# Attention steps in another order: scores three steps ahead, maxima turned one step earlier, the mask added by TensorE in 156 of 256 steps

## Chip, core and metric

The kernel runs on one core of one Trainium2 chip. The metric is the device time of one execution in microseconds (us): the time of the whole launch, of which the profile's span, from the first to the last instruction, is all but a microsecond or two. Smaller is better. A "granted clock" of 1.00 in the profile is TensorE at 2.4 GHz, 0.50 is 1.2 GHz.

## What is computed

The input `x` has 8 batches of 512 tokens with 512 features. A layer norm is followed by a cross attention with 16 heads of 32 features over a context of which the causal mask leaves the first 512 rows; then a second layer norm and a routed feed forward follow.

```python
def attention(q, latent_kv, Wq, Wkv_expand, Wout):      # per batch
    qp = q @ Wq.T
    k, v = jnp.split(latent_kv @ Wkv_expand.T, 2, axis=-1)
    scores = jnp.einsum('bhqd,bhkd->bhqk', qh, kh) * inv_sqrt_d
    scores = jnp.where(causal, scores, jnp.finfo(scores.dtype).min)
    attn = jax.nn.softmax(scores, axis=-1)
    out = jnp.einsum('bhqk,bhkd->bhqd', attn, vh)
    return out @ Wout.T

x = x + attention(layernorm(x), ctx, Wq, Wkv_expand, Wout)
x = x + ffn(layernorm(x))      # router softmax over 8 experts per output, two best, weighted
```

The change touches the attention alone.

## The kernel before

**Work and order.** Every engine has its program written out by hand; semaphores tie the programs together. The attention is a chain of 32 groups, four to a batch: group c of batch b (`n = 4b + c`) is four heads. A group has eight **steps** v = 0 to 7 (`UNITS`), and all five engines walk through the same steps. I call steps 0 to 4 the head of a group and steps 5 to 7 its tail. After the last group come the router and the experts, to which nothing is changed.

**Two passes of scores.** The softmax needs the maximum of each row before its exponentials. So the scores are computed twice. *First pass* (`scores`, L621): one step covers one block of 128 queries and two heads, and fills the two halves of the PSUM tile `pair0` (`s_ps`), one half a head. Widths go down as the steps of the target group go up: targets 0 and 1 are 512 keys wide, 2 and 3 are 384, 4 and 5 are 256, 6 and 7 are 128. VectorE (`maxima`, L1286) adds the mask tile `future` and takes the maximum in one custom instruction for each head, which is followed by an instruction that reads the accumulator into a column of `nmax`. The next use of a half waits for that (`negmax`). `target(c, v)` says for which step of a later group step v computes first-pass scores: `LEAD` = 2 steps ahead of one group's distance. So at step 5 the last scores (target 7) of group n+1 are issued, and at step 6 the first ones of group n+2.

**Turning the maxima.** When group n+1 has its 16 columns of maxima, TensorE turns them (`turn_maxima`, L630, into the PSUM tile `ps5`, which also holds the sums `d_ps`). ScalarE takes the rounded part (`hi_shift`, L964, `nm_h`), VectorE the rest (`lo_shift`, L1295, `nm_l`). SyncE puts both by DMA (L342) into two rows of the stack `qk_st` of group n+1. This happens at `TURN` = step 6. Step 0 of group n+1 waits for these rows (`rows_in`).

**Second pass** (`shifted_scores`, L648): keys by queries, two heads a step, into `pair1`, with the maximum already subtracted by those two rows. ScalarE takes the exponentials (L1023) into `pT`. GpSimd zeroes the diagonal's upper part (L1738, `causal`) and adds the blocks up for the sums (L1725, L1730, `added`). TensorE multiplies with the values (L661, step 6 and 7 and step 1 of the next group: `finish_group`) and forms the sums (L673, and L681 in `finish_group`, behind the last addition of GpSimd).

**Work of other kinds in the same steps.** Queries (steps 0, 2, 3, 4) and keys (`key_step`: step 5 for c = 0 and 3, step 6 for c = 1 and 2) are made three groups ahead, each in three matmuls (L262, L263, L264: high by high, low by high, high by low), and split by ScalarE (L956) and VectorE (L1270 queries, L1273 keys). In group 0 the values and the turning of the next batch's tokens (L570, L1261) come in. The output projection of the batch before, 16 chunks of three matmuls, lies at c = 1, 2 and 3 (`out_block`); after the fourth chunk of a token block VectorE adds the residual (L1322, `x1_ok`), and the next user of that PSUM bank waits for it. `refined` (L1301, L1303, step 3) and `scaled` (L1309, step 4) are VectorE's normalisation of the group before. `STATISTICS` are the steps in which VectorE takes the layer norm's statistics for two batches ahead (L1227) and GpSimd the scales from them (L1692 to L1702). `NORMALISED` are the steps in which ScalarE applies them (L988). `SPLIT` has ScalarE and GpSimd split the outputs (L971, L1683).

Batch 0 has no output projection, batches 1 to 6 are alike, and batch 7 has nothing ahead.

## Time and profile before

| | us |
|---|---|
| median of 3 runs | 2108.45 (2106.45 to 2109.36) |
| the profiled execution | 2109.9 |
| its span | 2108.2 |
| TensorE busy, and its share of the span | 2001.4 (95%) |
| VectorE, ScalarE, GpSimd busy | 1464.4, 1044.2, 851.9 |
| first to last second-pass step of the attention | 56.2 to 677.9 |
| batches 1 to 6 of the attention | 125.48 to 598.62, 473.14 in all, 78.86 each |
| from 677.92 to the end | 1430.28 |

The profile gives, for each engine, busy time and, for a group of like instructions, what ended the idle time before them. PE is TensorE, PEld its loading of weights, DVE is VectorE, ACT ScalarE, POOL GpSimd, SPq the issues of DMAs by SyncE. Matmuls overlap: one of 512 columns shows about 0.40 us, while the next begins 0.23 us after it; so a busy share near 100% is not the same as no time to gain, and starts are to be compared rather than durations.

### The profile page before, as it was taken

The numbers are of one execution on the slowest core, as the hardware profiler recorded it, in microseconds if no ns is written. First come the engines' busy times: TensorE is split into PE (matmuls) and PEld (weight loads), VectorE is DVE, ScalarE is ACT, GpSimd is POOL, SyncE is SP. The second block draws the span as 40 slices with busy tenths as digits, with TensorE's granted clock in tenths as the row PEclk, the third lists the DMA queues.
The fourth block names the chain that finished last, engine by engine and source line by source line (L and its number), as shares of the span: only waits on it lengthen the run. The fifth ranks groups of instructions, "written<-read, shape, count | busy, mean of one in ns | idle before, by whom it ended". The sixth has DMA issues, their size and how long they took to land.

```text
span 2108.2 us, 31128 instructions
## 1 busy us (share of the span) xinstructions
PE 2001.4 (95%) x9822; PEld 1522.9 (72%) x9872; DVE 1464.4 (69%) x3268; ACT 1044.2 (50%) x2093; POOL 851.9 (40%) x985
## 2 busy tenths in 40 slices
PE   5899998999986899999999999999999999999999
PEld 3566666665663677777777777778888888888887
DVE  5766666766665667777778777657877878778533
ACT  2665565565554246767676776733433334333300
POOL 3676666676666334435344345202311113111100
PEclk8999999999997999999999999999999999999999
DMA  5454454454353545455445455472322222222110
GB/s 155 117 126 111 131 130 112 130 135 115 102 148 120 192 159 204 162 192 184 164 175 207 150 189 187 154 269 81 109 95 75 77 92 93 106 80 75 60 40 31
DMA packets 99220, 275.85 MB, mean 131 GB/s; under 512 B 13435, under 2 KB 14480, under 8 KB 95030
## 3 DMA queue, kind: packets, MB, share of 16 engines
q1 hardware_dynamic: 94518, 216.16, 32.3%
q10 hardware_dynamic: 4608, 58.72, 8.1%
q14 instruction: 69, 0.57, 0.1%
q8 instruction: 25, 0.41, 0.1%
HBM read 131.67 MB, written 92.27 MB: 106 GB/s over the span
## 4 chain that ended last, share of the span: by engine, by line
PE 85%; DVE 4%; DMA 3%; POOL 2%; SPq 2%; issue 2%; ACT 1%; ACTq 0%; POOLq 0%; DVEq 0%
PE pair L262 21%; PE pair L264 20%; PE pair L263 20%; PE ps L262 3%; PE pair L621 3%; PE pair L648 3%; PE ps L661 3%; PE ps L264 3%; PE ps L263 3%; PE pair L859 2%; DVE pair L1286 1%; SPq L356 1%; DMA qk_st<-nm_l 1%; PE ps L681 1%; DVE xr L1322 1%
## 5 line engine op out<-in xcount | busy, mean ns | idle before, releaser
L262 PE MATMUL pair<-w_h,hT 128*128 128x512 f32 x1920 | 797.1, 415 | 3.5 <-DVE xb L1620 1.9
L264 PE MATMUL pair<-w_h,hT 128*128 128x512 f32 x1920 | 751.7, 392 | 0.0
L263 PE MATMUL pair<-w_l,hT 128*128 128x512 f32 x1920 | 747.6, 389 | 0.0
L1811 POOL TENSOR_TENSOR logits<-logits,second 128x512 f32<-128x512 f32 x224 | 298.4, 1368 | 609.0 <-DVE second L1499 608.7
L264 PEld LDWEIGHTS pair<-w_h,hT 128*128 128x128 f32 x1920 | 360.6, 188 | 80.2
L263 PEld LDWEIGHTS pair<-w_l,hT 128*128 128x128 f32 x1920 | 361.6, 188 | 74.7
L262 PEld LDWEIGHTS pair<-w_h,hT 128*128 128x128 f32 x1920 | 363.3, 189 | 71.4 <-issue 2.3
L1286 DVE CUSTOM_DVE_ANT_0 pair<-pair,future 128x256 f32<-128x256 f32 (+3 forms) x512 | 245.3, 508 | 159.5 <-PE pair L621 156.4
L1620 DVE SCALAR_TENSOR_TENSOR xb<-pair,c_now,xb 128x512 f32<-128x512 f32 x256 | 191.9, 750 | 190.4 <-PE pair L264 183.2
L1023 ACT ACTIVATE pT<-pair,zero 128x1024 f32<-128x1024 f32 (+3 forms) x256 | 202.4, 791 | 220.2 <-PE pair L648 212.3
L621 PE MATMUL pair<-qk_st 96*128 96x256 f32 (+3 forms) x512 | 164.5, 358 | 29.6 <-DVE nmax L1286 25.9
L1692 POOL TENSOR_TENSOR rstd<-moments,eps 128x1 f32<-128x1 f32 x64 | 33.0, 516 | 324.9 <-DVE moments L1237 297.1
L1738 POOL TENSOR_SCALAR_AFFINE_SELECT pT<-pT 128x256 f32<-128x256 f32 x256 | 109.0, 427 | 129.5 <-ACT pT L1023 129.5
L621 PEld LDWEIGHTS pair<-qk_st 96*128 96x128 f32 x512 | 101.1, 198 | 75.2 <-DVE nmax L1286 36.0
L1553 DVE SCALAR_TENSOR_TENSOR scrap<-ps,w 128x512 bf16<-128x512 f32 x224 | 153.2, 684 | 0.8 <-ACT w L1119 0.8
L648 PE MATMUL pair<-qk_st 98*128 98x256 f32 (+3 forms) x512 | 132.1, 342 | 22.2 <-DMA qk_st<-nm_l 16.8
L1092 ACT ACTIVATE over<-over 128x512 f32<-128x512 f32 x224 | 141.7, 633 | 7.1
L1547 DVE SCALAR_TENSOR_TENSOR ps<-logits,ps 128x512 f32<-128x512 f32 x192 | 133.3, 694 | 17.0 <-DVE scrap L1553 0.5
L1089 ACT ACTIVATE junk<-over 128x512 bf16<-128x512 f32 x224 | 141.5, 632 | 7.1
L1116 ACT ACTIVATE w<-tree 128x512 f32<-128x512 f32 x32 | 20.3, 633 | 239.7 <-DVE tree L1501 239.7
L1730 POOL TENSOR_TENSOR acc<-acc,pT 128x512 f32<-128x512 f32 (+1 forms) x124 | 128.7, 1038 | 10.3
L1084 ACT ACTIVATE over<-logits 128x512 f32<-128x512 f32 x224 | 129.6, 623 | 0.4
(166 smaller groups left out, 2784.0 us busy)
## 6 DMA issues: line engine op xcount, KB each, us to landing
logits<-lg_all ACTq DMA_DIRECT2D x32, 1792.0 KB, 7.5
qk_st<-qk SPq DMA_DIRECT2D x384, 128.0 KB, 2.3
lg_all<-ev_a SPq DMA_DIRECT2D x32, 768.0 KB, 5.6
lg_all<-ev_b SPq DMA_DIRECT2D x32, 768.0 KB, 3.3
xb<-x SPq DMA_DIRECT2D x64, 256.0 KB, 3.2
hT_all<-hT SPq DMA_DIRECT2D x32, 512.0 KB, 3.6
hT<-hT_all SPq DMA_DIRECT2D x32, 512.0 KB, 3.7
...
```

The costliest lines, as they stand in the source:

```text
L262: pe.matmul(dst, lh, rh, start=start, stop=False)
L263: pe.matmul(dst, lh, rl, start=False, stop=False)
L264: return pe.matmul(dst, ll, rh, start=False, stop=stop)
L621: pe.matmul(s_ps[:, j, 0:w], qk_st[c][0:STACK, 0, hh, i * P:w], qk_st[c][0:STACK, 1, hh, 0:w], start=True, stop=True).then_inc(s["scores"], 1)
L648: mm = pe.matmul(dst[:, j, 0:w], qk_st[c][0:STACK + SHIFT_ROWS, 1, hh, kb * P:(kb + 1) * P], qk_st[c][0:STACK + SHIFT_ROWS, 0, hh, kb * P: ...
L1023: act.activation(pT[kb][:, pair:pair + 2, :], src[:, :, 0:S - kb * P], ACT.Exp, bias=zero[:])\
L1089: act.activation(junk[:], over[j][:], ACT.Sign, accum_out=sign_sum[:, i, e:e + 1])\
L1092: act.activation(over[j][:], over[j][:], ACT.Tanh, scale=0.5, accum_out=tanh_sum[:, i, e:e + 1]).then_inc(s["first_step"], 1)
L1286: dve.tensor_tensor_reduce(row, row, future[:, S - (i + 1) * P:S], -1.0, -MASKED, ALU.add, ALU.min, accum_out=nmax[:, c % 2, at:at + 1]).t ...
L1553: dve.scalar_tensor_tensor(scrap[:, e % 2, :], taken_ps[e % 2], 1.0, w2[:], ALU.min, ALU.mult, accum_out=c_taken[:, i, e - 1:e]).then_inc( ...
L1620: dve.scalar_tensor_tensor(xb[i][:], l_ps[e % 4], c_now[i][:, e:e + 1], xb[i][:], ALU.mult, ALU.add).then_inc(s["acc"], 1)
L1811: pool.tensor_tensor(logits[t % 2][:, e - 1, :], logits[t % 2][:, e - 1, :], second[:], ALU.subtract)\
```

## The change

- `LEAD` goes from 2 to 3: first-pass scores run three steps ahead. The last of group n+1 (target 7) are issued at step 4, those of group n+2 begin at step 5.
- `TURN` goes from 6 to 5, and TensorE turns the maxima at the end of the step, behind that step's scores. ScalarE's `hi_shift` stays with it, behind a key split of the same step; VectorE's `lo_shift` comes at the beginning of step 6.
- In 156 steps (all eight with c = 0, steps 1 to 4 otherwise) the mask is added by TensorE: behind the score matmuls of both heads come two matmuls of 128 columns, one a head, with `ident_r` and `mask_r`, into the diagonal block. There both heads are issued together, and VectorE takes both maxima by one `tensor_reduce` over both halves. The other steps (5, 6, 7 and 0 with c = 1, 2, 3, targets 0 to 3) keep the custom instructions, with head 0 at the end of a step and head 1 in the next.
- The two halves of `refined` go to steps 3 and 4, `scaled` to the beginning of step 5. The keys for c = 0 and 3 are made right behind the second-pass scores of step 5, ahead of its scores.
- The output projection's blocks begin at (c, step) = (1, 0), (1, 6), (2, 3), (3, 0) instead of (1, 0), (1, 4), (2, 0), (3, 0) (unchanged in the last batch); the residual addition comes one step after the last chunk. One store of a sum goes from SyncE's part of c = 2 to that of c = 3.
- `STATISTICS` go from (1, 5), (2, 1), (2, 5), (3, 1) to (2, 1), (3, 0), (3, 1), (3, 2), and one of the normalisations from (2, 5) to (3, 6).

```diff
-LEAD = 2
+LEAD = 3
+        def masked(c, v):
+            return c == 0 or target(c, v)[1] >= QB
-        TURN = 6
+        TURN = 5
+        WEIGHTED = 6
-        STATISTICS = ((1, 5), (2, 1), (2, 5), (3, 1))
-        NORMALISED = ((2, 5), (3, 1), (3, 5), (3, 7))
+        STATISTICS = ((2, 1), (3, 0), (3, 1), (3, 2))
+        NORMALISED = ((3, 1), (3, 5), (3, 6), (3, 7))
-        SCALED = 4
+        SCALED = 5
+        OUT_FIRST = ((1, 0), (1, 6), (2, 3), (3, 0))
+        OUT_FIRST_LAST = ((1, 0), (1, 4), (2, 0), (2, 4))
...
-                    pe.matmul(s_ps[:, j, 0:w], ..., start=True, stop=True).then_inc(s["scores"], 1)
+                    mm = pe.matmul(s_ps[:, j, 0:w], ..., start=True, stop=not mask)
+                    if not mask:
+                        mm.then_inc(s["scores"], 1)
+                if mask:
+                    for j in heads:
+                        pe.matmul(s_ps[:, j, i * P:w], ident_r[:], mask_r[:], start=False, stop=True)\
+                            .then_inc(s["scores"], 1)
...
                 if some(n - 1):
-                    pe.wait_ge(s["o_ok"], n - 1)
+                    pe.wait_ge(s["refined"], 2 * (n - 1))
                 pe.transpose(r_ps, nmax[:, c % 2, :], ident[:]).then_inc(s["turned"], 1)
...
+                if mask:
+                    at = 2 * pair * QB + i
+                    dve.wait_ge(s["scores"], 2 * u + 2)
+                    dve.tensor_reduce(nmax[:, c % 2, at:at + QB + 1:QB], s_ps[:, :, 0:(i + 1) * P], AX_X, ALU.max,
+                                      negate=True).then_inc(s["negmax"], 2)
...
                     for v in range(UNITS):
-                        if v == TURN and (more or c < KC - 1):
+                        if v == TURN + 1 and (more or c < KC - 1):
                             lo_shift(n + 1)
-                        if v == key_step(c) == TURN and ahead:
+                        if not (first and c == 0) and v == SCALED:
+                            scaled(n - 1, (c - 1) % KC)
+                        if v == key_step(c) and ahead:
                             lo_of(n + AHEAD, KL, "k", key_bank(c))
...
-                            maxima(n + g, (c + g) % KC, vv)
+                            maxima(n + g, (c + g) % KC, vv, masked(c, v))
-                            if v == REFINED:
-                                refined(n - 1, (c - 1) % KC)
-                            if v == SCALED:
-                                scaled(n - 1, (c - 1) % KC)
+                        if not (first and c == 0) and REFINED <= v < REFINED + 2:
+                            refined(n - 1, (c - 1) % KC, v - REFINED)
```

**VectorE, group c = 3 of batch 5, from the last but one narrow maxima to the split of the turned ones.** In a row, `ISA` with 128x1 reads the accumulator, and `pair0,nmax` is the custom instruction. Before:

```order
L1286 ISA pair0,nmax_81<-pair0,future_84 128x128
L1286 ISA nmax_81 128x1
L1286 ISA pair0,nmax_81<-pair0,future_84 128x128
L1286 ISA nmax_81 128x1
L1309 TENSOR_TENSOR o_sb2_89<-ps4,o_sb2_89 128x512
L1270 SCALAR_TENSOR_TENSOR qk_72<-ps7,qk_72 128x512
L1286 ISA pair0,nmax_81<-pair0,future_84 128x128
L1286 ISA nmax_81 128x1
L1286 ISA pair0,nmax_81<-pair0,future_84 128x128
L1286 ISA nmax_81 128x1
L1273 TENSOR_TENSOR qk_72<-ps6,qk_72 128x512
L1295 TENSOR_TENSOR nm_l_83<-ps5,nm_h_82 16x128
```

and now, from the last narrow maximum (the `TENSOR_REDUCE`) on:

```order
L1305 TENSOR_REDUCE nmax_81<-pair0 128x2
L1350 TENSOR_TENSOR xr_96<-ps6,xr_96 128x512
L1331 SCALAR_TENSOR_TENSOR o_sb2_91<-ps5,o_sb2_91 128x512
L1290 SCALAR_TENSOR_TENSOR qk_72<-ps7,qk_72 128x512
L1337 TENSOR_TENSOR o_sb2_91<-ps4,o_sb2_91 128x512
L1293 TENSOR_TENSOR qk_72<-ps6,qk_72 128x512
L1311 ISA pair0,nmax_81<-pair0,future_84 128x512
L1311 ISA nmax_81 128x1
L1311 ISA pair0,nmax_81<-pair0,future_84 128x512
L1311 ISA nmax_81 128x1
L1320 TENSOR_TENSOR nm_l_83<-ps5,nm_h_82 16x128
```

Between the last maximum of a group and `nm_l` there was one key split; now the residual, the second half of `refined`, the query split, `scaled`, the key split and two maxima 512 wide stand there.

**TensorE, steps 5 and 6 of the same kind of group (c = 3, batch 6).** Before, from the end of step 4 on:

```order
L621 MATMUL pair0<-qk_st0_73 128x128 x2
L648 MATMUL pair1<-qk_st3_76 128x256 x2
L621 MATMUL pair0<-qk_st0_73 128x128 x2
L262 MATMUL ps6<-ctx_h_69,wkv_h_63 128x512
L263 MATMUL ps6<-ctx_l_70,wkv_h_63 128x512
L264 MATMUL ps6<-ctx_h_69,wkv_l_64 128x512
L648 MATMUL pair1<-qk_st3_76 128x128 x2
L661 MATMUL ps4<-pT0_77,v_sb_71 32x512 x4
L630 MATMUL ps5<-ident_49,nmax_81 16x128
```

and now:

```order
L634 MATMUL pair0<-qk_st0_73 128x128 x2
L640 MATMUL pair0<-mask_r_86,ident_r_85 128x128 x2
L667 MATMUL pair1<-qk_st3_76 128x256 x2
L265 MATMUL ps6<-ctx_h_69,wkv_h_63 128x512
L266 MATMUL ps6<-ctx_l_70,wkv_h_63 128x512
L267 MATMUL ps6<-ctx_h_69,wkv_l_64 128x512
L634 MATMUL pair0<-qk_st1_74 128x512
L649 MATMUL ps5<-ident_49,nmax_81 16x128
L667 MATMUL pair1<-qk_st3_76 128x128 x2
L634 MATMUL pair0<-qk_st1_74 128x512
L680 MATMUL ps4<-pT0_77,v_sb_71 32x512 x4
```

The keys stand ahead of the scores, the turn stands ahead of step 6's second-pass scores instead of behind its values, and the scores there are already those of the group after next.

**GpSimd, group c = 3 of batch 5, steps 1 to 3.** `AFFINE_SELECT` is the diagonal of a step, `rstd` and `nmean` the scales. Before:

```order
L1738 AFFINE_SELECT pT0_77<-pT0_77 128x2x128 x2
L1692 TENSOR_TENSOR rstd_53<-moments_52,eps_58 128x1
L1694 TENSOR_TENSOR rstd_53<-rstd_53,minus_half_57 128x1
L1699 TENSOR_TENSOR nmean_54<-moments_52,rstd_53 128x1
L1702 TENSOR_TENSOR nmean_54<-nmean_54,minus_one_55 128x1
L1738 AFFINE_SELECT pT1_78<-pT1_78 128x2x128
L1725 TENSOR_TENSOR acc_86<-pT0_77,pT1_78 128x768
L1738 AFFINE_SELECT pT1_78<-pT1_78 128x2x128
L1725 TENSOR_TENSOR acc_86<-pT0_77,pT1_78 128x768
```

and now, from step 1's scales on:

```order
L1719 TENSOR_TENSOR rstd_53<-moments_52,eps_58 128x1
L1721 TENSOR_TENSOR rstd_53<-rstd_53,minus_half_57 128x1
L1726 TENSOR_TENSOR nmean_54<-moments_52,rstd_53 128x1
L1729 TENSOR_TENSOR nmean_54<-nmean_54,minus_one_55 128x1
L1765 AFFINE_SELECT pT1_78<-pT1_78 128x2x128
L1752 TENSOR_TENSOR acc_88<-pT0_77,pT1_78 128x768
L1719 TENSOR_TENSOR rstd_53<-moments_52,eps_58 128x1
L1721 TENSOR_TENSOR rstd_53<-rstd_53,minus_half_57 128x1
L1726 TENSOR_TENSOR nmean_54<-moments_52,rstd_53 128x1
L1729 TENSOR_TENSOR nmean_54<-nmean_54,minus_one_55 128x1
L1765 AFFINE_SELECT pT1_78<-pT1_78 128x2x128
L1752 TENSOR_TENSOR acc_88<-pT0_77,pT1_78 128x768
```

A second set of scales stands between the two long additions (and a third one, not shown, between the diagonals of steps 0 and 1).

## Rows read from the trace of the kernel before

**Rows 1.** Busy time by stretch: heads and tails of batch 3, then batches 1 to 6.

```profile
core 0: us, PE busy (x) PEld busy (x) DVE busy (x) ACT busy (x) POOL busy (x), PEclk, DMA share, GB/s
285.64:296.89 11.25, 11.25 (x70) 8.55 (x70) 6.19 (x20) 7.96 (x11) 7.75 (x10) 1.00 0.80 210
296.89:304.20 7.31, 7.03 (x58) 4.58 (x58) 5.80 (x19) 4.86 (x11) 6.08 (x9) 1.00 0.09 20
304.20:316.84 12.64, 11.86 (x74) 8.75 (x72) 8.34 (x26) 7.11 (x10) 8.75 (x11) 1.00 0.76 202
316.84:323.96 7.12, 7.12 (x51) 4.56 (x50) 5.48 (x20) 2.50 (x5) 6.26 (x11) 1.00 0.26 86
323.96:335.79 11.83, 11.14 (x70) 8.28 (x69) 7.26 (x25) 5.96 (x8) 3.75 (x8) 1.00 0.67 167
335.79:344.12 8.33, 6.93 (x40) 4.09 (x40) 6.62 (x22) 3.73 (x7) 7.76 (x13) 0.80 0.10 36
344.12:354.99 10.87, 10.87 (x70) 8.36 (x69) 6.73 (x24) 6.67 (x9) 5.06 (x11) 1.00 0.62 144
354.99:363.85 8.86, 5.60 (x40) 2.79 (x40) 6.67 (x21) 5.59 (x11) 8.61 (x10) 1.00 0.12 39
125.48:598.62 473.14, 437.12 (x2761) 300.75 (x2761) 315.75 (x1020) 263.84 (x404) 325.26 (x456) 0.96 0.47 122
```

**Rows 2.** The waits of 125.48 to 598.62: in total, times, longest.

```profile
PE pair L621 <- DVE nmax L1286: 17.2, 15, 1.5
...
PE pair L648 <- DMA qk_st<-nm_l: 7.5, 8, 1.5
PE ps L262 <- DVE xr L1322: 6.9, 12, 0.7
```

**Rows 3.** Timeline of 282 to 364: start, duration, engine, line.

```profile
282.70 0.28 DVE L1295 TENSOR_TENSOR nm_l<-ps,nm_h 16x128 fp32r<-16x128 f32 x1 [1.17 <-ACT nm_h L964]
...
285.64 0.72 PE L648 MATMUL pair<-qk_st 98*128 98x512 f32 x2 [1.01 <-DMA qk_st<-nm_l]
...
356.40 0.29 DVE L1286 CUSTOM_DVE_ANT_0 pair<-pair,future 128x128 f32<-128x128 f32 x1
...
356.86 0.69 DVE L1309 TENSOR_TENSOR o_sb<-ps,o_sb 128x512 f32<-128x512 f32 x1
357.46 0.68 DVE L1270 SCALAR_TENSOR_TENSOR qk<-ps,qk 128x512 fp32r<-128x512 f32 x1
...
359.22 0.28 PE L630 MATMUL ps<-ident,nmax 128*16 128x128 f32 x1
...
360.52 0.28 DVE L1295 TENSOR_TENSOR nm_l<-ps,nm_h 16x128 fp32r<-16x128 f32 x1 [1.04 <-ACT nm_h L964]
360.73 0.68 DVE L1286 CUSTOM_DVE_ANT_0 pair<-pair,future 128x512 f32<-128x512 f32 x1
...
361.98 0.13 DVE L1286 DVE_READ_ACCUMULATOR2_ANT nmax<- 128x1 f32 x1
...
363.85 0.73 PE L648 MATMUL pair<-qk_st 98*128 98x512 f32 x2 [1.30 <-DMA qk_st<-nm_l]
```

**Rows 4.** Timeline of TensorE, 316 to 327: two narrow scores; a projection that waits.

```profile
316.67 0.34 PE L621 MATMUL pair<-qk_st 96*128 96x128 f32 x2
...
325.12 0.40 PE L264 MATMUL ps<-xnT_h,wq_l 128*128 128x512 f32 x1
326.21 0.50 PE L262 MATMUL ps<-wo_h,oT_h 128*128 128x512 f32 x1 [0.69 <-DVE xr L1322]
```

**Rows 5.** VectorE's groups by shape: count, busy, mean ns, idle before.

```profile
L1286 DVE CUSTOM_DVE_ANT_0 pair<-pair,future 128x512 f32<-128x512 f32 x128 | 87.0, 705 | 32.0 <-PE pair L621 31.8
```

**Rows 6.** Timeline of GpSimd in the last group of batch 3.

```profile
351.74 0.19 POOL L1692 TENSOR_TENSOR rstd<-moments,eps 128x1 f32<-128x1 f32 x1 [3.02 <-DVE moments L1237]
...
353.04 0.41 POOL L1738 TENSOR_SCALAR_AFFINE_SELECT pT<-pT 128x256 f32<-128x256 f32 x1
...
366.40 0.73 POOL L1730 TENSOR_TENSOR acc<-acc,pT 128x256 f32<-128x256 f32 x1
```

More of the change, by code:

```diff
@@ L606, in project_out, with scores @@
                     mm.then_inc(s["wo_mm"], 1)
-            def scores(n, c, v, heads=(0, 1)):
+            def scores(n, c, v, heads=(0, 1), mask=False):
                 u = n * UNITS + v
@@ L800, in body @@
                         if more or c + g < KC:
-                            scores(n + g, (c + g) % KC, vv, (0,) if vv < LATE else (0, 1))
-                        if v == key_step(c) != TURN and ahead:
-                            take(key_bank(c), "K", n + AHEAD)
-                            keys((c + AHEAD) % KC, b if c == 0 else b + 1, key_bank(c))
+                            if masked(c, v):
+                                scores(n + g, (c + g) % KC, vv, mask=True)
+                            else:
+                                scores(n + g, (c + g) % KC, vv, (0,))
+                        if v == TURN and (more or c < KC - 1):
+                            turn_maxima(n + 1, c + 1)
             def epilogue():
```

67 lines of the change are left out of this document (36 added, 31 removed).

## The prediction, as written before the changed kernel was run

> **What bounds the kernel now.** I read the stretches of batch 3 first [rows 1], then the waits [rows 2], then the timeline where the waits lie [rows 3, 4]. A batch of the attention takes 78.86 us in the mean of batches 1 to 6 (473.14 / 6), and TensorE is busy for 437.12 of those 473.14 [rows 1]: 36 us of gaps. What follows the attention, some 1430 us, isn't touched. So at most an eighth of the attention, and a fiftieth of the kernel, is open even if every gap goes, save for starts that lie further apart than a dense stream's.
>
> The gaps aren't spread evenly. The four heads (steps 0 to 4) of batch 3 take 11.25, 12.64, 11.83 and 10.87 us, with TensorE busy for 11.25, 11.86, 11.14 and 10.87; the tails (steps 5 to 7) take 7.31, 7.12, 8.33 and 8.86, with 7.03, 7.12, 6.93 and 5.60 [rows 1]. The reader is to see that the tails of c = 2 and 3 hold most of it, and that the granted clock is 0.80 in the tail of c = 2 and 1.00 in the others. The waits name three causes on TensorE: a first-pass score that waits for a maximum (17.2 us), second-pass scores that wait for the maxima's rows (7.5 us in 8 groups), and an output projection that waits for the residual (6.9 us, 12 times) [rows 2].
>
> The timeline shows how the tail of c = 3 ends: the turn at 359.22, the low half done at 360.80, second-pass scores at 363.85 with 1.30 us of idle time for the DMA [rows 3]. **The chain that ends a group is: last maximum, turn, split, two DMAs, next group.** From the end of the low half to the next group it took 3.05 us here and 2.66 a batch earlier (282.98 to 285.64, it waited there too) [rows 3]. I take 2.65.
>
> **Masks on TensorE.** A batch has 20 masked steps, 40 extra matmuls of 128 columns; 312 in all (7 x 40 + 32). Two scores of that width show 0.34 us together [rows 4], while one matmul of 128 moving columns shows 0.28 [rows 3]: so the second starts 0.06 us after the first. 312 x 0.06 = 19 us, 2.4 a batch, on TensorE's stream; nothing where it waits anyway, and 0.17 each (half of the pair's 0.34), 53 us, if they don't follow each other so closely. I take 0.06, since four narrow matmuls now stand in a row. On the other side stand scores one target later in each step: in a head two scores fall from 384 to 256 and two from 256 to 128, about -0.2 us at a column's rate (those of 512 start 0.23 us apart in a dense stream, as said under the profile above). Net per head: +0.25 for c = 1 to 3 (8 masks, 0.48, less 0.23), +0.37 for c = 0 (10 masks). In the tail of c = 0 it is +0.36 for masks and +0.23 for widths.
>
> The Trainium skill, page "TensorE: Matmul & The Clock Gate", section "Back-to-back issue gap", gives about 81 ns for a sustained matmul of 128 columns with its weight load. The rows show 60; by the page the masks would cost 25 us instead of 19.
>
> **Maxima by one instruction.** The trace has no `tensor_reduce`. The nearest rows: the custom instruction takes 0.29 us at 128 and 0.705 at 512 elements [rows 3, 5], so about 1.08 ns an element and 0.15 us fixed. Over both halves that is 0.43 us (2 x 128), 0.70, 0.98 and 1.26 (2 x 512). Today two narrow ones take 0.46 from start to the next start (356.40 to 356.86), two wide ones 1.25 and 0.13 (360.73 to 361.98, then the read) [rows 3]. In starts the gain is 0 to 0.15 us a step: at most 156 x 0.15 = 23 us of VectorE, which has a third of its time free [rows 1]. From above, twice the time per element adds 0.28 to a narrow and 1.1 to a wide one. I take the lower end, since unlike instructions of 512 fp32 elements from PSUM (L1309, L1270, L1286) all take 0.68 or 0.69 us there [rows 3].
>
> The Trainium skill, page "VectorE: DVE Perf Modes", section "Rules for kernel authors", speaks against this part: it calls `tensor_reduce` the slowest VectorE instruction, with a single rate of 1x, and advises to restructure around it. No row here shows it.
>
> **Tails.** Now the turn itself waits for nothing, but `nm_l` stands behind two wide maxima. The chain from the end of step 4 is VectorE's queue: end of the matmul 0.25, last narrow maxima 0.37, then `refined`, query split and `scaled` at 0.60 from start to start (356.86 to 357.46 [rows 3]), two wide maxima 1.25, `nm_l` 0.30: 3.97, and 2.65 of DMA: 6.6. The residual of c = 1 and c = 3 and the key split of c = 3 (and c = 0) add 0.60 each.
> - c = 0: chain 0.25 + 0.37 + 4 x 0.60 + 1.1 (both heads by one instruction) + 0.30 + 2.65 = 7.1; TensorE's own work 7.31 + 0.59 - 0.28 of gap [rows 1] = 7.6. It takes 7.6.
> - c = 1: chain 7.2; own work 7.12 - 0.69 (three of three projections become two) + 0.23 = 6.7. It takes 7.2.
> - c = 2: chain 6.6; own work as for c = 1, 6.7 (two projections, now at steps 5 and 6). It takes 6.7.
> - c = 3: chain 6.6 + 1.2 = 7.8; own work 6.7 less two projections of 0.69, 5.3. It takes 7.8.
>
> Together 29.3 us for 31.6 in batch 3. What is late next is thus VectorE's queue, no longer the wait of a narrow score behind `refined` (17.2 us in six batches), which goes.
>
> **Heads.**
> - c = 0: 11.25 + 0.37 + 0.6 = 12.2. The 0.6 is GpSimd: in batch 3 its last addition of c = 3 ends at 367.13 (366.40 + 0.73) [rows 6], 3.3 us after the next group began, and just when `finish_group` wants it. One more set of scales (351.74 to 353.04, 1.30 us [rows 6]) now stands between the long additions. The two steps before GpSimd's additions have slack, so I put half of the 1.3 on the path.
> - c = 1: 12.64 - 0.69 (step 4's projection) - 0.6 (its wait, 6.9 / 12 [rows 2]) + 0.25 = 11.6.
> - c = 2: 11.83 - 0.86 (the projection's wait, 325.12 to 326.21 less 0.23 [rows 4]) + 0.25 + 0.45 = 11.7. The 0.45 is a new wait: block 2 begins at step 3 behind the residual of step 2 (0.25 + 0.60 + 0.69 + 0.05 = 1.6 after step 2's scores, while TensorE is there after 1.15).
> - c = 3: 10.87 + 0.25 + 0.8 = 11.9. The same wait moves here: block 3 begins at step 0, the residual of block 2 stands behind the maximum of head 1, whose score is issued in that same step 0. Queued behind the waiting projection on TensorE are the first head's score of step 0 and all of step 1.
>
> Together 47.4 for 46.6. **Sum:** 47.4 + 29.3 = 76.7 for 78.86: 2.2 us a batch, 13 in six. Batch 0 has no projection and batch 7 nothing ahead; I put nothing there. The constants `ident_r` and `mask_r` cost GpSimd less than a us while it waits for the first loads. Span 2108.2 - 13 = 2095; the profiled execution (2109.9) lies 1.5 above the median of the runs, 2108.45, so against that median 2095 as well.
>
> **Rivals.**
> - *TensorE's own work becomes the bound.* If VectorE's queue is shorter than I add up, and the residual and GpSimd hold nobody, heads are 11.6 + 11.6 + 11.2 + 11.1 = 45.5 (those above without the 0.6, 0.45 and 0.8) and tails 7.6 + 6.7 + 6.7 + 5.3 = 26.3: 71.8, 7.0 us a batch, 42 in all: 2066. For it: the granted clock of 0.80 in one tail [rows 1] comes back with the gaps. Against: seven VectorE instructions at 0.60 are plain in the new order. Half of what this rival adds would give 2080.
> - *GpSimd ends the last group (slower).* All three sets of scales of 1.3 us now stand in c = 3, behind three statistics for which GpSimd must wait (3.02 us for one today [rows 6]), in front of additions that already end when TensorE asks for them. Two sets more, 2.6, and 1.4 of waiting, all passed on at step 1 of group 0: +4.0 - 2.2 = +1.8 a batch, 11 in all: 2119. It decides as soon as the last addition ends later than 3 us after the next group's begin by more than the tails have gained.
> - *The turn at step 5 brings nothing.* The low half sits behind two wide maxima, and if `tensor_reduce` runs at half the rate of the custom instruction (+0.28 in four chains, +1.1 in c = 0, 2.2 a batch), the gain is used up: 2108. The Trainium skill's rule on `tensor_reduce`, above, points this way.
>
> **How the numbers follow.** Forecast 2095 (2086 to 2106): 0.42. TensorE-bound, 2066 to 2085: 0.18. GpSimd-bound, 2110 to 2125: 0.23. Nothing, 2104 to 2112: 0.17. About 0.2%, 4.2 us, is what a measurement of this kernel tells from no change. Faster: 0.18 + 0.36 of the forecast's 0.42 + 0.03 = 0.57. Same: 0.04 + 0.10 + 0.01 = 0.15. Slower: 0.22 + 0.02 + 0.04 = 0.28. The range that leaves out 0.1 on each side is 2074 to 2119.
>
> **What the changed profile would show.** Batches 1 to 6 at about 76.7 us each, their tails near 7.6, 7.2, 6.7 and 7.8. `nm_l` some 4 to 5.2 us behind the end of step 4, with wide maxima right ahead of it. Waits of first-pass scores for maxima down from 17.2 to a few us; second-pass scores that still wait for the rows. Projection waits in c = 2 step 3 and c = 3 step 0 only. The mask matmuls 0.06 us apart. A `tensor_reduce` of 2 x 128 at 0.43 us. GpSimd's last addition of c = 3 about 0.5 us late. The forecast is wrong if a batch's time changes in the heads rather than in the tails, or if the end of a group hangs on ScalarE, which takes one more normalisation at c = 3, step 6, or on GpSimd.

## The result, and the profile after

The changed kernel takes **2134.73 us** (median of 4 runs, 2127.21 to 2138.16) where the kernel before takes 2108.9 (4 runs): a ratio of **1.0116**, 95% interval 1.0085 to 1.0148. It is slower, beyond the forecast's upper end (2106) and beyond every range that was given a chance (2125). The profiled execution took 2136.3 (span 2134.6). From the last second-pass step (703.95) to the end it is 1430.65 us, for 1430.28 before: the loss is all in the attention. There 1.3 us come before its first step, 1.3 in batch 0, 1.3 in batch 7, and 22.2 in batches 1 to 6 (495.36 for 473.14, 82.56 a batch for 78.86).

Busy time by stretch of the changed kernel: heads and tails of batch 3, then batches 1 to 6 (columns and order as in [rows 1]; the granted clock stands third from the end).

```profile
295.74:308.79 13.05, 12.29 (x80) 9.31 (x80) 4.00 (x7) 8.03 (x12) 10.11 (x14) 1.00 0.71 181
308.79:316.85 8.06, 7.49 (x65) 5.48 (x64) 6.78 (x11) 5.26 (x11) 6.32 (x9) 1.00 0.11 25
316.85:328.46 11.61, 11.46 (x78) 8.87 (x78) 5.60 (x11) 6.20 (x9) 7.33 (x9) 1.00 0.81 210
328.46:338.51 10.05, 8.55 (x47) 4.62 (x47) 6.27 (x15) 3.01 (x6) 6.04 (x9) 0.83 0.21 67
338.51:350.51 12.00, 11.85 (x78) 9.00 (x78) 6.29 (x16) 6.50 (x8) 4.96 (x10) 1.00 0.60 144
350.51:357.70 7.19, 6.63 (x48) 3.86 (x47) 5.59 (x14) 2.48 (x5) 6.48 (x9) 1.00 0.11 36
357.70:369.87 12.17, 11.60 (x78) 9.00 (x77) 7.82 (x24) 6.66 (x9) 5.75 (x15) 1.00 0.62 152
369.87:377.67 7.80, 5.86 (x41) 2.90 (x41) 6.80 (x17) 6.25 (x12) 7.39 (x10) 1.00 0.10 36
...
128.04:623.40 495.36, 457.07 (x3001) 319.93 (x3001) 291.77 (x660) 263.93 (x404) 325.91 (x458) 0.97 0.45 117
```

Two stretches stand out: the head of c = 0 (13.05) and the tail of c = 1 (10.05, granted clock 0.83). The head of c = 0 is 13.69 in the mean of six batches, because batch 1 takes 16.87 there, at a granted clock of 0.80:

```profile
128.04:144.91 16.87, 15.07 (x79) 11.10 (x80) 4.00 (x7) 8.24 (x12) 11.54 (x15) 0.80 0.54 140
```

The means of batches 1 to 6, beside the forecast:

| | heads c = 0, 1, 2, 3 | tails c = 0, 1, 2, 3 | batch |
|---|---|---|---|
| before | 11.76 12.60 11.83 10.89 | 7.29 7.16 8.38 8.96 | 78.86 |
| forecast | 12.2 11.6 11.7 11.9 | 7.6 7.2 6.7 7.8 | 76.7 |
| after | 13.69 11.58 11.99 12.19 | 8.06 10.05 7.24 7.77 | 82.56 |

The waits of TensorE in batches 1 to 6 (in total, times, longest):

```profile
PE ps L680 <- DVE o_sb L1337: 9.8, 18, 0.6
PE ps L265 <- DVE xr L1350: 8.8, 13, 0.9
...
PE ps L649 <- DVE o_sb L1331: 4.2, 6, 0.7
PE ps L680 <- POOL pT L1765: 3.9, 6, 1.7
```

The wait that the forecast wanted gone is gone (first-pass scores for maxima, 17.2 us in [rows 2], now 1.8 in two rows). In its place stands one that the forecast doesn't name: the values' product (L680, step 6), 18 times, which is once in each of c = 0, 1 and 2 of six batches, waits for `scaled` (L1337). The timeline of the tail of c = 1 shows it (start, duration, engine, line, shape, idle before):

```profile
329.07 0.68 DVE L1350 TENSOR_TENSOR xr<-ps,xr 128x512 f32<-128x512 f32 x1
...
329.67 0.68 DVE L1331 SCALAR_TENSOR_TENSOR o_sb<-ps,o_sb 128x512 f32<-128x512 f32 x1
330.27 0.68 DVE L1290 SCALAR_TENSOR_TENSOR qk<-ps,qk 128x512 fp32r<-128x512 f32 x1
...
330.41 0.28 PE L649 MATMUL ps<-ident,nmax 128*16 128x128 f32 x1 [0.70 <-DVE o_sb L1331]
...
330.87 0.68 DVE L1337 TENSOR_TENSOR o_sb<-ps,o_sb 128x512 f32<-128x512 f32 x1
331.46 0.69 DVE L1311 CUSTOM_DVE_ANT_0 pair<-pair,future 128x512 f32<-128x512 f32 x1
331.69 1.93 PE L680 MATMUL ps<-pT,v_sb 128*32 128x512 f32 x8 [0.55 <-DVE o_sb L1337]
...
333.56 0.80 PE L265 MATMUL ps<-ctx_h,wkv_h 128*128 128x512 f32 x1
```

The values of step 6 go into the PSUM tile `ps4`, which `scaled` of the group before still reads. Before, `scaled` ran at the end of step 4; now it is at 330.87 behind the residual, the second half of `refined` and the query split, and TensorE stands. The turn, too, waits for `refined`. Between the two waits TensorE has three small jobs, and then its clock is down: the eight value products take 1.93 us here, for 1.06 at full clock (e1_scaled4, below). The stretches around it, and the same place one batch earlier and one later:

```profile
329.50:331.60 2.10, 0.94 (x5) 0.42 (x4) 2.10 (x5) 0.99 (x3) 2.02 (x3) 1.00 0.32 125
331.60:335.10 3.50, 3.41 (x12) 1.49 (x13) 1.39 (x5) 0.00 (x0) 1.93 (x3) 0.51 0.26 82
335.10:338.50 3.40, 3.40 (x28) 2.22 (x27) 2.01 (x5) 1.07 (x2) 1.14 (x2) 1.00 0.16 36
...
249.80:253.20 3.40, 3.40 (x12) 1.45 (x13) 1.26 (x5) 0.00 (x0) 1.81 (x3) 0.50 0.26 82
...
413.60:417.00 3.40, 3.34 (x12) 1.42 (x13) 1.36 (x5) 0.00 (x0) 1.91 (x3) 0.50 0.31 82
```

TensorE was busy for 0.94 of 2.10 us, and the next 3.4 us run at 1.2 GHz: in every one of batches 1 to 6, at the same place. The kernel before has such stretches too: in the tail of c = 2 in five of the six batches, in that of c = 3 in four, and once in the head of c = 0. In all they are 37.5 us long there and 27.3 us in the changed kernel, so the mean clock of batches 1 to 6 is 0.96 before and 0.97 after.

GpSimd at the end of c = 3 of batch 2 and the head of c = 0 of batch 3, with the TensorE rows that wait for it:

```profile
297.13 0.40 POOL L1765 TENSOR_SCALAR_AFFINE_SELECT pT<-pT 128x256 f32<-128x256 f32 x1
297.62 0.73 POOL L1757 TENSOR_TENSOR acc<-acc,pT 128x256 f32<-128x256 f32 x1
298.31 1.27 POOL L1710 TENSOR_TENSOR oT_l<-o_sb,oT_h 128x512 fp32r<-128x512 f32 x1
299.55 0.40 POOL L1765 TENSOR_SCALAR_AFFINE_SELECT pT<-pT 128x256 f32<-128x256 f32 x1
300.03 0.73 POOL L1757 TENSOR_TENSOR acc<-acc,pT 128x256 f32<-128x256 f32 x1
```
```profile
300.08 0.43 PE L680 MATMUL ps<-pT,v_sb 128*32 128x128 f32 x8 [0.45 <-POOL pT L1765]
300.81 0.85 PE L700 MATMUL ps<-acc,ones 128*32 128x384 f32 x8 [0.31 <-POOL acc L1757]
```

GpSimd has no gap there. Its last addition ends at 300.76, 5.0 us after the group began (295.74), where it was 3.3 before [rows 6]. In batch 1 the values wait 1.67 us for GpSimd at this place, and the next 6.8 us run at 1.2 GHz.

### The profile page after: what moved, and what is told of

Same layout as the page of the kernel before. It is cut to its first block, busy times and chain, and to the rows that moved or that the text cites. A ratio compares the mean times of both kernels' runs of the same rounds, so it can differ in the third digit from the quotient of the medians.

```text
span 2134.6 us, 31419 instructions
## 1 busy us (share of the span) xinstructions
PE 2026.5 (95%) x10134; PEld 1548.6 (73%) x10184; DVE 1431.8 (67%) x2800; ACT 1044.2 (49%) x2093; POOL 852.6 (40%) x987
## 4 chain that ended last, share of the span: by engine, by line
PE 82%; POOL 6%; DVE 5%; issue 2%; DMA 2%; SPq 1%; ACT 1%; POOLq 0%; DVEq 0%; ACTq 0%
PE pair L265 21%; PE pair L267 20%; PE pair L266 20%; PE ps L265 3%; PE ps L680 3%; PE pair L634 3%; PE pair L667 2%; PE ps L266 2%; PE ps L267 2%; PE pair L879 2%; POOL oT_l L1710 1%; POOL acc L1757 1%; POOL acc L1752 1%; POOL pT L1765 1%; PE pair L640 1%
## 5 line engine op out<-in xcount | busy, mean ns | idle before, releaser
L1305 DVE TENSOR_REDUCE nmax<-pair 128x2 f32<-128x256 f32 (+3 forms) x156 | 104.2, 668 | 175.6 <-PE pair L640 175.4
L634 PE MATMUL pair<-qk_st 96*128 96x256 f32 (+3 forms) x512 | 150.5, 346 | 16.8 <-DVE nmax L1311 9.7
L1311 DVE CUSTOM_DVE_ANT_0 pair<-pair,future 128x512 f32<-128x512 f32 (+3 forms) x200 | 121.2, 627 | 49.6 <-PE pair L634 48.0
L667 PE MATMUL pair<-qk_st 98*128 98x256 f32 (+3 forms) x512 | 135.4, 347 | 14.8 <-DMA qk_st<-nm_l 11.9
L634 PEld LDWEIGHTS pair<-qk_st 96*128 96x128 f32 x512 | 95.9, 194 | 67.8 <-DVE nmax L1311 21.5
```

The source lines that it names most:

```text
L634: mm = pe.matmul(s_ps[:, j, 0:w], qk_st[c][0:STACK, 0, hh, i * P:w], qk_st[c][0:STACK, 1, hh, 0:w], start=True, stop=not mask)
L667: mm = pe.matmul(dst[:, j, 0:w], qk_st[c][0:STACK + SHIFT_ROWS, 1, hh, kb * P:(kb + 1) * P], qk_st[c][0:STACK + SHIFT_ROWS, 0, hh, kb * P: ...
```

## Experiments

Each kernel is the changed one with the edit shown, unless it says otherwise. Names like `SCALED` are those of the diff above. All are compared with the kernel before, run on the same chip. The means of batches 1 to 6 of each profiled execution:

| | heads c = 0, 1, 2, 3 | tails c = 0, 1, 2, 3 | batch | time | ratio (95%) |
|---|---|---|---|---|---|
| e1_scaled4 | 13.32 11.57 11.98 12.19 | 7.42 7.57 6.56 8.04 | 78.65 | 2110.2 | 1.0010 (0.9998 to 1.0021) |
| e2_stats | 12.05 11.58 11.98 12.26 | 8.06 9.21 7.31 7.76 | 80.22 | 2123.64 | 1.0073 (1.0056 to 1.0091) |
| e3_blocks | 13.63 12.73 12.17 11.35 | 8.06 7.89 7.33 7.60 | 80.75 | 2124.12 | 1.0082 (1.0062 to 1.0101) |
| e4_nomask | 13.79 10.78 11.27 11.50 | 7.89 8.47 7.18 7.88 | 78.76 | 2111.11 | 1.0014 (1.0002 to 1.0026) |
| e5_scaled_stats | 12.11 11.57 12.08 12.28 | 7.42 7.66 6.78 8.03 | 77.93 | 2107.14 | 0.9999 (0.9988 to 1.0011) |
| e12_masks_custom | 12.06 11.55 12.03 12.26 | 7.41 7.84 6.64 8.16 | 77.96 | 2107.09 | 1.0000 (0.9990 to 1.0009) |
| e9_all_three | 11.57 10.84 11.37 11.58 | 7.08 7.88 6.77 8.60 | 75.68 | 2092.24 | 0.9927 (0.9901 to 0.9953) |
| e8_lead_turn | 11.81 11.71 11.51 10.73 | 7.20 7.31 7.78 7.92 | 75.97 | 2094.84 | 0.9942 (0.9925 to 0.9959) |
| e10_apart | 11.85 11.25 11.37 11.58 | 6.89 7.88 6.66 8.69 | 76.17 | 2092.93 | 0.9931 (0.9915 to 0.9948) |
| e13_residual | 11.99 10.80 11.05 10.74 | 7.30 8.33 6.93 7.96 | 75.09 | 2088.3 | 0.9908 (0.9883 to 0.9934) |
| e11_filler | 13.72 11.57 11.98 12.18 | 8.06 8.54 7.21 7.77 | 81.02 | 2128.34 | 1.0102 (1.0077 to 1.0128) |

### One part undone at a time

**e1_scaled4**: VectorE's normalisation at its old place.

```diff
-SCALED = 5
+SCALED = 4
-    if not (first and c == 0) and v == SCALED:        # at the step's beginning
-        scaled(n - 1, (c - 1) % KC)
-    if not (first and c == 0) and REFINED <= v < REFINED + 2:
-        refined(n - 1, (c - 1) % KC, v - REFINED)
+    if not (first and c == 0):                        # at its end
+        if v == REFINED:
+            refined(n - 1, (c - 1) % KC, 0)
+            refined(n - 1, (c - 1) % KC, 1)
+        if v == SCALED:
+            scaled(n - 1, (c - 1) % KC)
```

> The changed kernel with one part undone: both halves of `refined` at step 3 and `scaled` at the end of step 4, as before, instead of steps 3, 4 and the beginning of 5. Theory V (the values of step 6 wait for `scaled`, which now stands behind the residual, `refined` and the query split; with the hole the granted clock falls in the tail of c = 1 in every batch): the tail of c = 1 goes from 10.05 to 7.2 to 7.5 us, those of c = 0 and 2 lose about 0.5 each, 3.5 to 3.9 a batch, 21 to 23 in all: about 2112. Theory P (GpSimd's additions end the last group late, head of c = 0): that head stays at 13.7 and the time falls by no more than 3. Theory M (the masks on TensorE): no change beyond 3 us.

It takes the ratio from 1.0116 to 1.0010; only e4_nomask has as large an effect. The tail of c = 1 falls by 2.5 us and those of c = 0 and 2 by 0.6 and 0.7. The timeline of the same place (e1_scaled4, batch 3):

```profile
319.96 0.68 DVE L1350 TENSOR_TENSOR xr<-ps,xr 128x512 f32<-128x512 f32 x1
...
320.43 0.27 PE L649 MATMUL ps<-ident,nmax 128*16 128x128 f32 x1
...
320.56 0.68 DVE L1337 TENSOR_TENSOR o_sb<-ps,o_sb 128x512 f32<-128x512 f32 x1
...
321.38 1.06 PE L680 MATMUL ps<-pT,v_sb 128*32 128x512 f32 x8 [0.22 <-DVE o_sb L1337]
```

The turn waits for nothing, the values for 0.22 us, and the clock stays: their eight products take 1.06 us. In batches 1 to 6 the wait of L680 for `scaled` is down from 9.8 to 1.1 us. The four tails are now 7.42, 7.57, 6.56 and 8.04, 29.6 together; the forecast had 29.3.

**e2_stats**: statistics and normalisations as before.

```diff
-STATISTICS = ((2, 1), (3, 0), (3, 1), (3, 2))
-NORMALISED = ((3, 1), (3, 5), (3, 6), (3, 7))
+STATISTICS = ((1, 5), (2, 1), (2, 5), (3, 1))
+NORMALISED = ((2, 5), (3, 1), (3, 5), (3, 7))
```

> The changed kernel with the layer norm statistics and normalisations of before: (1,5), (2,1), (2,5), (3,1) and (2,5), (3,1), (3,5), (3,7). Theory P: GpSimd's last addition of c = 3 ends 1.3 us sooner after the next group's begin, the head of c = 0 goes from 13.7 to 12.2, 1.5 a batch, 9 in all: about 2125; the tail of c = 1 stays near 10, or grows by 0.9 since a statistic returns to its step 5. Theory V or M: within 3 us of the changed kernel.

The head of c = 0 falls from 13.69 to 12.05: 1.64 us in the mean. In batches 2 to 6 it is 1.2 us (13.05 to 11.87), in batch 1, where the clock no longer falls, 3.9. The last addition ends 3.7 us after the group began (297.51 and 293.77), and TensorE follows it without a wait:

```profile
296.78 0.73 POOL L1757 TENSOR_TENSOR acc<-acc,pT 128x256 f32<-128x256 f32 x1
```
```profile
297.71 0.83 PE L700 MATMUL ps<-acc,ones 128*32 128x384 f32 x8
```

The tail of c = 1 also falls in the mean (10.05 to 9.21), though nothing in it is changed: the clock drops in two of the six batches there instead of six, with the same two waits in all of them. In batch 3, at full clock, it takes 8.47.

**e3_blocks**: projections and residual at their old places.

```diff
-OUT_FIRST = ((1, 0), (1, 6), (2, 3), (3, 0))
+OUT_FIRST = ((1, 0), (1, 4), (2, 0), (3, 0))
-            step = c * UNITS + v - (0 if last else 1)
+            step = c * UNITS + v
```

> The changed kernel with the output projection's blocks of before (beginning at (1,0), (1,4), (2,0), (3,0), residual in the step of the last chunk). Theory C (moving two projections out of steps 4 and 5 of c = 1 leaves the hole in which the granted clock falls; the wait for `scaled` alone costs only its own 0.6): the granted clock stays 1.00 in the tail of c = 1 and that tail, with one projection more, falls from 10.05 to about 8.9; the waits for the residual return in the heads of c = 1 and 2 (+0.6 and +0.4): net -0.2 to 0 a batch, 2134 to 2136. Theory V with the wait itself as the whole cause: the tail of c = 1 gets 0.7 longer by the projection, 10.7, and the total is 4 to 10 us slower.

With a third projection in it the tail of c = 1 takes 7.89 instead of 10.05, although it has more to do: the clock stays at 1.00. The turn no longer waits for `refined` either, since the projection stands in that hole; the values still wait 0.55 us for `scaled`. So this run isn't one of the clock alone. The expectations (8.9 for this tail, 2134 to 2136 in all) were too high: the kernel takes 2124.12.

```profile
323.71:331.62 7.91, 7.36 (x51) 4.42 (x50) 5.67 (x14) 2.48 (x5) 5.04 (x7) 1.00 0.25 66
```

**e4_nomask**: no masks by TensorE; both heads of a step are still issued together in those steps, and each maximum is taken by the custom instruction.

```diff
                             if masked(c, v):
-                                scores(n + g, (c + g) % KC, vv, mask=True)
+                                scores(n + g, (c + g) % KC, vv)
...
-                            maxima(n + g, (c + g) % KC, vv, masked(c, v))
+                            maxima(n + g, (c + g) % KC, vv)
```

> The changed kernel without mask matmuls: the masked steps issue their two score matmuls together as now, and VectorE adds the mask and takes the maximum by the custom instruction for each head. Theory M (the masks are what makes it slower): 312 x 0.06 to 0.09 us of TensorE go, 19 to 28 us faster, 2107 to 2116. Theories V and P: TensorE has room in the tails, and only the dense heads gain, 0.4 to 0.6 each in four heads less what the two custom instructions cost VectorE: 0 to 8 us faster, and the tail of c = 1 and the head of c = 0 keep most of their excess.

The heads of c = 1, 2 and 3, with 8 masks each, are shorter by 0.80, 0.72 and 0.69: 0.09 to 0.10 us a mask. A pair of narrow steps' matmuls shows the same, with masks (changed kernel) and without (e9_all_three, below):

```profile
286.17 0.34 PE L634 MATMUL pair<-qk_st 96*128 96x128 f32 x2
286.34 0.39 PE L640 MATMUL pair<-mask_r,ident_r 128*128 128x128 f32 x2
286.56 0.45 PE L667 MATMUL pair<-qk_st 98*128 98x256 f32 x2
```
```profile
269.20 0.34 PE L634 MATMUL pair<-qk_st 96*128 96x128 f32 x2
269.37 0.45 PE L667 MATMUL pair<-qk_st 98*128 98x256 f32 x2
```

From the scores to what follows it is 0.39 with the two masks and 0.17 without: 0.11 each at this place.

The ratio goes from 1.0116 to 1.0014, as far as the theory on the masks had it (2107 to 2116, measured 2111.11) and beyond the 8 us of the others. But not all of this is the masks' own time. Of the 3.80 us a batch, 1.58 are in the tail of c = 1: the clock falls there in one batch of six, although the turn waits 0.9 us and the values 0.55. The head of c = 0 isn't shorter, because in batches 3 to 6 the clock now falls in it, behind a wait of 1.4 us for GpSimd. It takes 14.23 in batch 3, and 12.44 in batch 2, at a clock of 1.00:

```profile
282.74:296.97 14.23, 12.51 (x69) 9.36 (x70) 4.71 (x19) 8.18 (x11) 10.70 (x13) 0.88 0.65 166
```

### Parts together

**e5_scaled_stats** has the edits of e1_scaled4 and e2_stats.

> The changed kernel with two parts undone together: `refined` and `scaled` at steps 3 and 4 as before, and the statistics and normalisations of before. If the two causes are separate (V: the values of step 6 wait for `scaled`; P: GpSimd ends the last group late), heads and tails add up: e1's 78.65 us a batch less the 1.3 that e2 took off the head of c = 0 give 77.3, some 8 us under e1: about 2102. If they are one (both runs only freed the same stretch from the low clock): no less than 2108.

The ratio is 0.9999: with both faults mended, the change is worth nothing. The clock stays at 1.00 in all of batches 1 to 6, where the kernel before has 0.96. The expectation was 0.6 a batch and 5 us too low. The two edits overlap in the tail of c = 1, where either takes away much of the lost clock (2.48 us by e1_scaled4, 0.84 by e2_stats, 2.39 by both), so their single effects can't be added. Beside e1_scaled4 the head of c = 0 is 1.2 us shorter and a batch 0.72; the intervals of the two ratios overlap.

**e9_all_three** adds the edit of e4_nomask.

> As e5, and without mask matmuls (custom maxima in all steps). What is left of the change is LEAD 3, TURN 5, the early keys and the new places of the projection. Theory M as a cause of its own (a mask costs TensorE 0.09 us in the dense heads, 0.7 to 0.8 a head, 3 a batch): 77.3 - 3.0 = 74.3 a batch, 18 under e5: about 2084. If the masks cost only together with the low clock of the tail of c = 1: no more than 5 under e5.

Ratio 0.9927. So the masks alone are worth 2.25 us a batch, where 3.0 were expected, and the difference of the two times on the same chip is 15 us, where 18 were.

**e12_masks_custom** asks what of that is the masks and what `tensor_reduce`: as e5_scaled_stats, but with custom maxima.

```diff
-                            maxima(n + g, (c + g) % KC, vv, masked(c, v))
+                            maxima(n + g, (c + g) % KC, vv)
```

> As e5_scaled_stats (refined whole at step 3, scaled at the end of step 4, statistics as before, masks by TensorE in 156 steps), but the maxima of those steps are taken by the custom instruction of before, one a head, which adds the mask a second time (the outputs don't change by that, since a masked score stays far below the others). Against e9_all_three it has only the mask matmuls more; against e5_scaled_stats only another way to take the maxima. Theory: what the masks cost, 2.25 us a batch between e5_scaled_stats and e9_all_three (77.93 and 75.68), is TensorE's 40 matmuls, not tensor_reduce: it stays at 77.9 (77.5 to 78.4) a batch and 2107 (2103 to 2111). Rival: a good part of it is tensor_reduce, which reads both heads at once and so can begin only when both are written: then a batch takes 76.5 or less, and the time is 2098 or less.

77.96 a batch for 77.93 and a ratio of 1.0000 for 0.9999: which instruction takes the maxima makes no difference, and all 15 us are TensorE's 312 small matmuls, 0.05 us each in the mean. From e12_masks_custom to e9_all_three the four heads get shorter by 2.54 us together, the tail of c = 0 by 0.33, and the other tails longer by 0.61.

**e8_lead_turn** adds the edit of e3_blocks to e9_all_three: what is left of the change is `LEAD`, `TURN`, the early keys, the heads issued together and the moved store.

> As e9, with the projection's places of before as well: only LEAD 3, TURN 5 and the early keys are left of the change (and in c = 0 both heads' scores stand together). If scores three steps ahead and the earlier turn are worth what the tails of c = 2 and 3 show in e1 (8.4 to 6.6, 9.0 to 8.0), heads stay as before and tails fall by 3: 76 a batch, about 2091 (2084 to 2098). If they are worth nothing by themselves: 2106 to 2111.

Ratio 0.9942, and 75.97 a batch, as expected. The tails of c = 2 and 3 are 0.6 and 1.0 us shorter than before (7.78 and 7.92 for 8.38 and 8.96). In c = 2 that is the clock: before, it fell in this tail in five of six batches, here in one. In the one batch where the clock was 1.00 the tail was shorter before (batch 4, first line) than it is here (batch 3, second line):

```profile
413.96:421.22 7.26, 5.47 (x39) 2.89 (x39) 6.36 (x21) 3.62 (x7) 6.78 (x11) 1.00 0.11 40
326.94:334.69 7.75, 5.68 (x39) 2.83 (x39) 7.55 (x23) 3.51 (x7) 7.18 (x13) 1.00 0.01 3
```

First-pass scores still wait for maxima here, 13.2 us in 23 places (17.2 in 15 before); with the projection at its new places it is 4.3 (e9_all_three, below). In c = 3 the tail is shorter at full clock too (7.56 for 8.86 in batch 3).

**e10_apart** lets c = 0 issue the heads of its wide steps apart again, on top of e9_all_three.

```diff
-            return c == 0 or target(c, v)[1] >= QB
+            return target(c, v)[1] >= QB
```

> As e9_all_three (no masks by TensorE, refined whole at step 3, scaled at the end of step 4, statistics as before), but in the group c = 0 the two heads of a wide step are again issued apart, head 0 at the end of a step and head 1 in the next, as before. Theory: with head 1 of step 0 behind the second-pass scores, TensorE has work while VectorE reads the first half; the tail of c = 0 (7.08) and its head (11.57) give up 0.1 to 0.3 together: 75.5 a batch, 2091. Rival: with the heads apart, the chain to the turned maxima waits for the second custom instruction one step later, and the tail of c = 0 grows by 0.3 to 0.6 us: 76.1, 2095.

Neither came true: the tail of c = 0 is 0.19 shorter, the heads of c = 0 and 1 are 0.28 and 0.41 longer (the 0.28 nearly all in batch 2, where the clock falls), and the time is the same (2092.93 for 2092.24). What lengthens the head of c = 1 wasn't looked into.

**e13_residual** takes one half of e3_blocks, on top of e9_all_three: the residual in the last chunk's step, the blocks where the change has them.

```diff
-            step = c * UNITS + v - (0 if last else 1)
+            step = c * UNITS + v
```

> As e9_all_three (no masks by TensorE, refined whole at step 3, scaled at the end of step 4, statistics as before), but the residual addition comes in the step of the last chunk, as before, instead of one step later; the blocks begin where the changed kernel has them. In e9_all_three the projections and key products still wait for the residual in 12 places of six batches, 11.0 us in all (1.8 us a batch), up to 1.4 us in step 5 of c = 3, where the key product shares the bank. Theory: with the residual a step earlier these waits go down to some 0.5 us a batch; half of what they give up is taken by VectorE's queue in the same step, whose maximum comes 0.6 us later: 75.0 a batch (0.7 less than the 75.68 of e9_all_three), 2088 (2084 to 2091). Rival: c = 3's end hangs on the chain from VectorE's last maxima to the DMA and not on this wait, and the narrow scores now wait for a maximum behind the residual, as they did before the change: no gain, 75.7 to 76.2, 2092 to 2095.

75.09 a batch and 2088.3 us, as expected. The waits of TensorE in e9_all_three, then in e13_residual, batches 1 to 6:

```profile
PE ps L265 <- DVE xr L1350: 11.0, 12, 1.4
PE pair L667 <- DMA qk_st<-nm_l: 6.8, 8, 2.4
PE pair L634 <- DVE nmax L1311: 4.3, 11, 0.7
```
```profile
PE pair L634 <- DVE nmax L1311: 12.0, 18, 1.3
PE pair L667 <- DMA qk_st<-nm_l: 10.2, 9, 2.1
```

The wait for the residual is gone altogether. All of the 11.0 us come back in these two rows (7.7 and 3.4), and still the six batches are 3.5 us shorter (0.59 each). The heads of c = 2 and 3 and the tail of c = 3 are shorter by 0.3, 0.8 and 0.6, the other stretches longer, the tail of c = 1 by 0.45 because the clock falls in it in batches 5 and 6. Why the exchange of one wait for others gains was not settled. **This kernel is the fastest of all here, 0.9908 of the time before**; its interval overlaps with those of e9_all_three and e10_apart.

### The clock by itself

**e11_filler**: the changed kernel, with useless matmuls of 512 columns in the two holes of c = 1 (batches 1 to 6).

```diff
+            def fill(count):
+                for _ in range(count):
+                    pe.matmul(j_ps[0][:], wo_h[:, 0, 0:P], wo_h[:, 0, :], start=True, stop=True)
...
+                            if c == 1 and more and not first:
+                                fill(2)            # ahead of the values, step 6
                             values_of(n, c, b, 0)
...
+                            if c == 1 and more and not first:
+                                freed(*held[0])
+                                fill(3)            # ahead of the turn, step 5
                             turn_maxima(n + 1, c + 1)
```

> The changed kernel with useless matmuls in the hole of c = 1, in batches 1 to 6: three of 512 columns ahead of the turn of step 5 and two ahead of the values of step 6, into a PSUM bank that is free there, 1.15 us of work in waits of about 1.3 us. Nothing of the computation is left out. Theory C (it is the low granted clock behind the hole that makes the tail of c = 1 10 us long): the clock stays 1.00 there, the tail falls by about 1.5 us, 9 in all, 2126, though work was added. If only the wait counts: the same or up to 3 us slower than the changed kernel, 2134 to 2138.

The tail of c = 1 falls from 10.05 to 8.54 with five matmuls more in it, and its clock is 1.00:

```profile
325.26:333.82 8.56, 8.22 (x53) 4.88 (x52) 6.26 (x15) 3.02 (x6) 6.12 (x9) 1.00 0.28 79
```

So of the 2.5 us between the changed kernel and e1_scaled4 in this tail, 1.5 are the clock and 1.0 the waits themselves (8.54 against 7.57). In e2_stats the same tail with the same waits takes 8.48 where the clock stays. In the time of the whole the filler's gain isn't settled: the intervals of 1.0116 and 1.0102 overlap.

## Why the prediction was wrong

**The forecast's order of parts.** The ratios lie on one path: 0.9927 (order of scores, turn, keys and blocks), plus 0.0072 for the masks (e9_all_three to e5_scaled_stats, 15 us), plus 0.0011 for the statistics (to e1_scaled4, 2 us, not clear of noise), plus 0.0106 for the place of `refined` and `scaled` (to the changed kernel, 22 us). Another order gives other shares: with `scaled` late the statistics cost 0.0043, 9 us, and the masks, taken out of the changed kernel as it is, 0.0102, 21.5 us. The parts don't simply add.

A batch was forecast at 76.7 and took 82.56. Of the 5.9 us between them 3.8 are in the tails (2.85 in that of c = 1) and 2.05 in the heads (1.5 in that of c = 0). A small part of the forecast's gain was never there: its stretches are added up from batch 3, which had 46.6 and 31.6, together 78.2, but the sum is set against the mean of 78.86. In its own terms the gain was 1.5 a batch, 9 us, not 2.2 and 13. (The gaps of 36 us are a thirteenth of the 473.14, not an eighth; nothing in the sum uses that.)

**The step that failed: the tails, and in them c = 1.** The sum put `scaled` into VectorE's chain to `nm_l` and asked when that chain ends. It didn't ask who else waits for `scaled`. On TensorE it is the values of step 6, by their PSUM tile. Before, in the tail of c = 1 of batch 3, `scaled` ended at 318.20 and the values began at 318.52, so no wait stands in the old trace, and the forecast, which read the waits that were there, missed the one that the move makes. `scaled` began 0.7 us after the tail did (316.84); now it is 2.4 us (330.87 and 328.46). The forecast counted what the move does to VectorE's queue and not who needs the result. Its price is 0.55 us in each of c = 0, 1 and 2 and a further 0.7 at the turn of c = 1, where the second half of `refined` is late in the same way. With both back at their old places the four tails take 29.6 (e1_scaled4), for 29.3 forecast. The chain that the forecast did add up was right where it ends the group: in the tail of c = 3 of batch 3 of the changed kernel

```profile
374.73 0.27 DVE L1320 TENSOR_TENSOR nm_l<-ps,nm_h 16x128 fp32r<-16x128 f32 x1
...
377.67 0.73 PE L667 MATMUL pair<-qk_st 98*128 98x512 f32 x2 [0.87 <-DMA qk_st<-nm_l]
```

the low half ends at 375.00, 5.1 us after the tail began, and 2.67 later (2.65 forecast) the next group starts: 7.80 for 7.8.

**The granted clock.** The forecast named the clock only as something to be got back. In the tails of c = 2 and 3 it was, and over batches 1 to 6 the changed kernel has less time at the low clock than the kernel before. But it fell where the forecast had no term for it. The change leaves TensorE idle for 1.2 of 2.1 us at one place of every batch, in a tail from which it also took a projection, and TensorE then runs 3.4 us at half speed: 1.5 us a batch. Filling the hole (e11_filler), putting a projection back (e3_blocks) or taking the waits away (e1_scaled4) each keep the clock there in all six batches, and other statistics (e2_stats) or no masks (e4_nomask) in four and five of them. The gain of e9_all_three over the kernel before, 15 us, holds what the clock gives back: 37.5 us at the low clock before, 6.8 with it. How much of the 15 us that is was not measured apart.

**GpSimd, the rival that was right in kind.** The forecast put 0.6 us on the head of c = 0 for the sets of scales in c = 3, the rival 4.0. It is 1.6 in the mean (e2_stats), 1.2 in five batches and 3.9 in the first, where the clock falls. "Half of the 1.3" was the mis-sized term: the last addition ends 5.0 us after the group began, and 3.7 in e2_stats, so one whole set of scales, 1.3 us, is passed on. The rival's 4.0 was too much; why the rest isn't passed on wasn't looked into. Its mark, a last addition later than 3 us after the group begins, was passed by 2 us.

**The masks, at the right total for the wrong reason.** The forecast took 0.06 us each, 2.4 a batch and 19 us in all, and they cost 2.25 and 15 (e12_masks_custom and e9_all_three), so with the two other faults mended they miss nothing in the sum. That is luck: the places that have masks cost 2.87 a batch, 0.5 more than the 2.4 of the forecast, and without the masks the tails of c = 1, 2 and 3, which have none, get 0.6 longer. The 0.06 came from the difference of two durations (0.34 for a pair, 0.28 for one). Between e12_masks_custom and e9_all_three the heads of c = 1, 2 and 3 differ by 0.71, 0.66 and 0.68 for 8 masks: 0.08 to 0.09 each, and 0.09 to 0.10 in e4_nomask. Starts would have told the dense price: the pair of scores at 286.17 is followed by the masks at 286.34, 0.085 us for each, and in the trace of before the pair at 316.67 [rows 4] is followed at 316.84. The Trainium skill, page "TensorE: Matmul & The Clock Gate", section "Back-to-back issue gap", gives about 81 ns, and the measurement in the dense heads agrees with it, and not with the price that I preferred.

**What was right.** `tensor_reduce`, by shape, over both halves (count, busy, mean ns, idle before):

```profile
L1305 DVE TENSOR_REDUCE nmax<-pair 128x2 f32<-128x512 f32 x62 | 43.0, 693 | 98.3 <-PE pair L640 98.2
...
L1305 DVE TENSOR_REDUCE nmax<-pair 128x2 f32<-128x256 f32 x62 | 26.4, 426 | 63.4 <-PE pair L640 63.3
L1305 DVE TENSOR_REDUCE nmax<-pair 128x2 f32<-128x1024 f32 x16 | 19.5, 1217 | 0.9 <-PE pair L640 0.9
```

0.43, 0.69 and 1.22 us, for 0.43, 0.70 and 1.26 estimated. The rule of the Trainium skill (page "VectorE: DVE Perf Modes", section "Rules for kernel authors"), by which `tensor_reduce` is the slowest instruction, makes no difference here: it reads PSUM at the rate of the custom instruction (0.71 us for 512), and e12_masks_custom shows that the time doesn't depend on it. The heads of c = 1 (11.58 for 11.6), c = 2 and c = 3 (0.3 above the forecast, of which the masks' price can be 0.2), the two new waits of projections (13 times, 8.8 us for 7.5) and the end of the old wait came as written. The other rival, TensorE's own work as the bound, is far off: even e13_residual, the best kernel, takes 75.09 a batch where it had 71.8.
